# Two copies on ScalarE ahead of the exponentials of the third slot, and a group's mean behind the feed-forward products on TensorE

## The reference, cut to what matters

```python
def shift_tokens(t):
    a, s = jnp.split(t, 2, -1)
    s = jnp.pad(s, ((0, 0), (1, 0), (0, 0)))[:, :-1]
    return jnp.concatenate([a, s], -1)
...
def ffn_layer(x, g, bln, W1, b1, W2, b2):
    mu = x.mean(-1, keepdims=True)
    var = ((x - mu) ** 2).mean(-1, keepdims=True)
    xn = (x - mu) / jnp.sqrt(var + 1e-05) * g + bln
    hg = xn @ W1 + b1
    a, gate = jnp.split(hg, 2, -1)
    return a * jax.nn.gelu(gate, approximate=False) @ W2 + b2
for i in range(DEPTH):
    x = attn_layer(shift_tokens(x), Wqkv[i], q_scale[i], k_scale[i], Wo[i]) + x
    x = ffn_layer(shift_tokens(x), ln_g[i], ln_b[i], W1[i], b1[i], W2[i], b2[i]) + x
```

## Time and profile before

| what | us |
|---|---|
| median of 3 runs | 3920.88 |
| lowest and highest run | 3917.01 and 3927.07 |
| profiled execution, its own time | 3918.71 |
| span of its instructions | 3916.9 |
| TensorE busy in the span | 3581.4 (91%) |
| VectorE busy | 3162.1 (81%) |
| ScalarE busy | 2652.5 (68%) |
| GpSimd busy | 2432.0 (62%) |

### The profile page before, as it was taken

One profiled execution on the slowest core, in us unless ns is written; L12 is line 12 of the kernel. 1 busy time (PEld: TensorE's weight loads), 2 busy tenths in 40 slices (PEclk: granted clock), 3 DMA queues, 4 the chain that ended last, 5 costly groups with the idle time before them and its releaser, 6 DMA issues.

```text
span 3916.9 us, 146395 instructions
## 1 busy us (share of the span) xinstructions
PE 3581.4 (91%) x60128; PEld 2226.2 (57%) x60128; DVE 3162.1 (81%) x4377; ACT 2652.5 (68%) x4972; POOL 2432.0 (62%) x2197
## 2 busy tenths in 40 slices
PE   5676776899999999999999999999999999999997
PEld 2222222566666666666666666666666666666664
DVE  4899998888878778888878788778787887888884
ACT  3555554677777777767776777677777777676765
POOL 0355554876666666666666666666666666666661
PEclk9889898999999999999999999999999999999999
DMA  3000000111111111111110111111111111110101
GB/s 76 0 0 0 0 0 0 34 32 31 31 42 41 34 30 31 31 47 38 35 32 26 42 42 36 32 31 31 45 37 33 31 31 47 36 36 27 32 28 37
DMA packets 64418, 120.05 MB, mean 31 GB/s; under 512 B 18196, under 2 KB 35986, under 8 KB 63634
## 3 DMA queue, kind: packets, MB, share of 16 engines
q1 hardware_dynamic: 63762, 110.70, 9.7%
HBM read 20.50 MB, written 2.10 MB: 6 GB/s over the span
## 4 chain that ended last, share of the span: by engine, by line
PE 53%; DVE 15%; issue 9%; ACT 7%; POOL 0%; ACTq 0%; DMA 0%; DVEq 0%; POOLq 0%; SPq 0%
PE ob L1187 10%; PE qk L1129 9%; PE sc L1214 7%; PE trb L1001 6%; PE vob L1195 4%; PE vob L1135 4%; PE sc L1163 4%; DVE arena L888 3%; PE sc L1221 3%; DVE ssq L894 3%; DVE mx L901 3%; PE ob L1001 2%; DVE arena L889 2%; ACT arena L619 2%; DVE xnT L978 1%
## 5 line engine op out<-in xcount | busy, mean ns | idle before, releaser
L507 POOL TENSOR_TENSOR arena<-arena,rnorm 128x512 f32<-128x512 f32 x768 | 793.7, 1054 | 929.3 <-ACT rnorm L626 928.8
L500 POOL TENSOR_TENSOR arena<-arena 128x512 f32<-128x512 f32 x768 | 961.7, 1274 | 84.9 <-DVE arena L889 84.9
L633 ACT ACTIVATE arena<-trb 128x512 f32<-128x512 f32 x768 | 465.7, 606 | 432.4 <-PE trb L1001 432.4
L1129 PE MATMUL qk<-wqkv,xs 128*128 128x512 f32 x1536 | 734.2, 601 | 16.0 <-issue 8.9
L888 DVE TENSOR_TENSOR arena<-qk,tab_q 128x512 f32<-128x512 f32 x384 | 263.7, 687 | 504.6 <-ACT arena L619 499.6
L483 POOL TENSOR_TENSOR arena<-arena 128x512 f32<-128x512 f32 x256 | 299.9, 1180 | 345.4 <-DVE arena L858 329.9
L1001 PE MATMUL trb<-ident,arena 128*128 128x128 f32 x3072 | 483.0, 280 | 10.7 <-ACT arena L633 7.6
L619 ACT ACTIVATE arena<-qk 128x512 f32<-128x512 f32 x768 | 433.5, 592 | 79.4 <-PE qk L1129 65.5
L1129 PEld LDWEIGHTS qk<-wqkv,xs 128*128 128x128 f32 x1536 | 294.5, 193 | 312.0 <-issue 294.8
L894 DVE TENSOR_REDUCE ssq<-arena 128x16 f32<-128x1024 f32 x384 | 464.3, 1209 | 0.0
L514 POOL TENSOR_TENSOR arena<-arena,rinv 128x512 f32<-128x512 f32 x384 | 392.4, 1043 | 65.8 <-DVE rinv L911 65.8
(11 more groups left out here) (139 smaller groups left out, 6020.5 us busy)
## 6 DMA issues: line engine op xcount, KB each, us to landing
arena<-arena SPq DMA_DIRECT2D x192, 384.0 KB, 3.2
arena<-arena SPq DMA_DIRECT2D x192, 64.0 KB, 3.0
wqkv<-in_L_ffn_Wqkv SPq DMA_DIRECT2D x18, 512.0 KB, 4.3
wo<-in_L_ffn_Wo SPq DMA_DIRECT2D x6, 512.0 KB, 4.0
arena<-in_L_attn_x SPq DMA_DIRECT2D x8, 256.0 KB, 2.8
out<-arena SPq DMA_DIRECT2D x8, 256.0 KB, 2.2
w<-in_L_ffn_W SPq DMA_DIRECT2D x6, 341.0 KB, 2.9
arena<-in_sel SPq DMA_DIRECT2D x1, 1024.0 KB, 5.0
```

Of the source, the lines that this page charges most:

```text
L500: nc.gpsimd.tensor_tensor(ts[c * 2 + j][:, heads], tu[:, 0, heads], tu[:, 1, heads], ALU.add).then_inc(summed[0], 1)
L507: nc.gpsimd.tensor_tensor(part, part, rnorm[j][:, 8 * h:8 * h + 8].unsqueeze(2).to_broadcast([P, 8, HEAD]), ALU.mult) \
L633: A((qT, kT)[j][u][:, 4 * h:4 * h + 4, at_col:at_col + P], TRB.rearrange("p (a t) -> p a t", a=4), ACT.Copy) \
L1129: MM(QK[:, 512 * h:512 * h + 512], lhsT=xs[u][:, c * P:(c + 1) * P], rhs=wqkv[:, col:col + 512], start=True, stop=True) \
```

## The change

Two things move, and no instruction is added or removed. On ScalarE, the copies for the next sequence (slots 2 and 6) move from the end of their slot to ahead of the exponentials of the same slot, and the copies for the norm, which ended slot 1, move to the same place in slot 2. On TensorE, the mean of slot 3 moves from ahead of the slot's up products to behind them. Its waits move with it.

```diff
@@ scalar engine, layer_slot
                 if up0 or up1:
                     act_e.preload_act_table_set(EXP_LN_SET)
+                if k % UNITS == 2:
+                    at_ = unit_at(l, k, -2)
+                    if at_:
+                        stage_x(at_[1], at_[2], (k + 2) // UNITS % BATCH, l + (k + 2) // LAYER)
+                    at_ = group_at(l, k - 1, LAG_STAGE)
+                    if at_:
+                        stage_norm(*at_)
                 at_ = step_at(l, k, LAG_SCORES)
                 if at_:
                     exps(*at_)
                 if unit:
                     norms(*unit)
-                at_ = unit_at(l, k, -2)
-                if at_ and (k + 2) % UNITS == 0:
-                    stage_x(at_[1], at_[2], (k + 2) // UNITS % BATCH, l + (k + 2) // LAYER)
-                at_ = group_at(l, k, LAG_STAGE)
-                if at_:
-                    stage_norm(*at_)
@@ tensor engine, layer_slot
                 mean = group_at(l, k, LAG_MEAN)
-                if mean:
-                    pe.wait_ge(ln_in[0], mean[1] + 1)
-                    if out_before:
-                        item(pe, x_added, out_before[0])
-                    MM(VOB[:, :], lhsT=meanw[:], rhs=xs2.rearrange("p s t -> p (s t)"), start=True, stop=True).then_inc(ln_mean[0], 1)
...
                         up(*at_, parts, scored)
+                if mean:
+                    pe.wait_ge(ln_in[0], mean[1] + 1)
+                    if out_before:
+                        item(pe, x_added, out_before[0])
+                    MM(VOB[:, :], lhsT=meanw[:], rhs=xs2.rearrange("p s t -> p (s t)"), start=True, stop=True).then_inc(ln_mean[0], 1)
```

## The result

The changed kernel takes 3821.22 us (median of 4 runs, 3817.41 to 3822.02) against 3922.95 us for the kernel before, measured beside it: 0.974 of it, with a 95% interval from 0.9723 to 0.9757. The direction and the main mechanism held; a second gain of a third of the whole was not foreseen.

What follows compares the result with a forecast made beforehand. TensorE, busy 64.53 of each 65.96 us period, was taken as the bound; 46 waits of 1.48 us give 68 us off 3918.71, 3850.7, or 3853 for the median. The range was 3845 to 3880 us.

Steps and rivals of the forecast that it cites:

- the main mechanism: Slot 3: with the mean behind the up products and ScalarE's copies moved, TensorE's wait goes, 46 x 1.48 = 68 us.
- What bounds the kernel: Whole period: TensorE, busy for 64.53 of 65.96 us, so only 1.43 us can be had from its waits.
- the mean's wait: Slot 3: TensorE sat idle before the mean for VectorE's addition L918, 46 times for 57.7 us; this would go.
- The 0.23 us beyond the mark: Slot 3: the wait costs TensorE 1.50 us, 0.23 more than the 1.27 of idle time shown in its timeline.
- the second rival: Slot 3: only the marked idle time goes and the 0.23 us stays: 57.7 us, 3863 us; chance 0.07.
- ScalarE's cover: Slot 2: ScalarE's 2.00 us of idle time before the exponentials hides the four copies, 2.15 us, almost exactly.
- The margin of the v product: Slot 3: L955 frees the bank in time for the v product, by 0.13 us to minus 0.02; no wait taken.
- the first rival: Slot 3: the v product waits 0.52 us for L955, 46 times; 24 us given back, 3877 us; chance 0.20.
- Slot 6: Slot 6: copies delay exponentials and norms by 0.87 us, but VectorE's sums start later anyway; counted as nothing.
- The wait of 0.17 us in slot 7 stays: Slot 7: TensorE's idle time of 0.17 us before the up products remains, with nothing gained there.
- The layers' borders: Slots at the layer's borders, where weights arrive, might lose what the others win; no size given.

Runs made afterwards that it cites:

- TensorE's part alone: Against the kernel before, only the mean moved behind the up products, ScalarE's list untouched: 3886.09 us against 3921.37, 0.9909.
- the copies moved alone: Against the kernel before, only the copies for the next sequence moved ahead of the exponentials in slots 2 and 6: 3889.34 us against 3922.16, 0.9913.
- GpSimd's wait alone: Against the kernel before, GpSimd's scaling in slot 6 waits until VectorE has written the normalised x; nothing else moved: 3892.83 us, 0.9921.
- the collision put back: Against the changed kernel, the norms of slot 6 placed ahead of the exponentials, so GpSimd's scaling again starts near VectorE's tensor_scalar: 3853.26 us, 0.9816.

## Why the prediction was wrong, point by point

**What bounds the kernel, and the mean's wait: right.** 46 x 1.48 = 68 us was forecast for slot 3, and 68.6 measured (1.50 us in the medians, 9.67 and 8.17). The 0.23 us beyond the mark were real, so the second rival falls.

**ScalarE's cover: right.** The copies took 2.16 us against 2.15. Relative to TensorE's q and k products of slot 3 the exponentials start 0.13 us earlier than before (1.25 us behind them instead of 1.38), where I had reckoned with 0 to 0.14 later: L663 starts 0.14 us before L633 ends. Between the copies themselves the rows still show no overlap (L671 starts 0.65 us after L670, which takes 0.63). So the 93 ns that the Trainium skill gives ("ScalarE: Activation LUTs", section "What ACT_TABLE_LOAD costs") does not hold among these copies; at their front, behind a copy out of PSUM, the overlap is 0.14 us. VectorE's idle time before the rotation of slot 2 fell from 3.27 to 1.98 us (medians over the groups), by the 1.29 us that the moved copies take; the 4.20 and the 2.9 that the prediction named belong to a group with an unusually long idle time, as the 1.62 shown above belongs to one with a short one.

**The margin of the v product: right in sign, somewhat larger.** 0.46 us from L956's end to the product, where 0.14 are needed. TensorE's part alone, without that margin, pays the first rival's price: a wait of 0.47 us a group, 21 us, where 0.52 and 24 were forecast. Slot 3 loses 25.6 of its 68.6 us there, but the other 4 are stops that the rival did not have.

**Slot 6: wrong, and this is the step that failed.** The sum put a term at nothing, "I count slot 6 as nothing", and asked only who would be late if the norms came 0.87 us later, and found nobody. It did not ask what a later start would no longer collide with. "The wait of 0.17 us in slot 7 stays" followed from it. The row was to be had: L978 with 1.36 us, and the same instruction without GpSimd beside it at 0.49 in the last two groups. The term is worth 20 us, and brought the long ends (8 to 10) with it: shown by the copies moved alone, by GpSimd's wait alone, and by the collision put back.

**The mark again.** A wait of 0.17 us in the timeline cost 0.43 a group. I had measured this excess for the mean and did not apply it to slot 7; 10.8 us of marked idle time before the up products (46 times) were worth 20.

**The layers' borders: wrong by omission.** I left room for them to lose. They won: 8 us in the long ends. Another 4.8 us lie in slot 0, mostly behind the loop's edge. That sum scatters from 383 to 390 us over the kernels of the table and the experiments without a pattern that I could find, so part of it may be chance of the profiled executions.

## What to carry to other kernels

When a step that releases another engine is moved, ask not only who waits for it but what that engine will then run beside. A later start on an engine with slack can be a gain, and a wait added on purpose can be one: 29 us came from a single semaphore wait on GpSimd. Where the same instruction has two durations in one trace, 0.49 and 1.29 us here, look for what ran beside the longer one; here it was GpSimd, and the line's least and median time side by side showed it.

## What the runs showed of the hardware that I had not expected

A VectorE tensor_scalar of 128 x 512 fp32, from SBUF to SBUF, takes 0.49 us, and 1.15 to 1.36 us when a GpSimd instruction starts within 0.3 us ahead of it or 0.03 us behind; it then ends 0.28 us after GpSimd's, in all 46 groups of the kernel before. TensorE can stop in the middle of its products without a semaphore, for 0.2 to 1.4 us, and each such stop here ends 1.22 to 1.61 us after a 16 KB instruction packet. At the layers' ends these stops come only where a 512 KB transfer and a wait of TensorE of 0.4 us fall into the same slot; elsewhere some come without the transfer, nearly all of them in TensorE's part alone. After the stop shown, the granted clock is 0.66 on average over the next 2.8 us, where it was 1.00 before it.
